# Attention kernel, one core: values of four heads in one go from a ring of five turned heads, and the inverse of the row sums spread on GpSimd

## The reference

```python
q, k, v = (proj(Wq), proj(Wk), proj(Wv))                   # x @ W.T, split into 16 heads of 32
scores = jnp.einsum('bhsd,bhtd->bhst', q, k) * D ** -0.5
scores = jnp.where(mask[None, None, :, :], -jnp.inf, scores)
attn = jax.nn.softmax(scores, axis=-1)
out = jnp.einsum('bhst,bhtd->bhsd', attn, v)
out = out.transpose(0, 2, 1, 3).reshape(B, S, E) @ Wo.T
xn = out / jnp.sqrt(jnp.mean(out * out, -1, keepdims=True) + EPS) * rms_scale
xn = xn * (1.0 + sc[:, None, :]) + shift[:, None, :]       # shift, sc from the condition
x = x + xn
x = x + x_rotated                                          # hamilton(q_left, hamilton(filtered x, conj q_right))
```

## Time and profile before

| | before |
|---|---|
| median of 3 runs | 988.27 us (987.57 to 989.47) |
| span of the profiled execution | 986.2 us |
| PE busy | 912.2 us (92%), 6278 matmuls |
| DVE busy | 707.5 us (72%) |
| ACT busy | 638.8 us (65%) |
| POOL busy | 523.6 us (53%) |
| mean granted TensorE clock | 0.979 |
| DMA | 153.98 MB, mean 156 GB/s |

### The profile page before, as it was taken

One profiled execution on the slowest core, in us unless ns is written; L12 is line 12 of the kernel. 1 busy time (PEld: TensorE's weight loads), 2 busy tenths in 40 slices (PEclk: granted clock), 3 DMA queues, 4 the chain that ended last, 5 costly groups with the idle time before them and its releaser, 6 DMA issues.

```text
span 986.2 us, 20466 instructions
## 1 busy us (share of the span) xinstructions
PE 912.2 (92%) x6278; PEld 648.2 (66%) x6278; DVE 707.5 (72%) x1581; ACT 638.8 (65%) x1523; POOL 523.6 (53%) x441
## 2 busy tenths in 40 slices
PE   7999999999968989999999998999999999999980
PEld 5788888888845557666666665666666666666650
DVE  4522132223168888989999898899999899898878
ACT  5222222223158888888888887788888888888820
POOL 0999930000001122677666776566677666776665
PEclk9999999999979999999999999999999999999995
DMA  8855465544878547756666745666665576455111
GB/s 282 303 188 193 170 223 189 183 171 181 186 249 185 118 98 181 164 117 151 150 140 139 194 108 129 152 155 145 142 161 125 133 187 156 109 120 139 33 54 43
DMA packets 82325, 153.98 MB, mean 156 GB/s; under 512 B 8472, under 2 KB 9112, under 8 KB 82224
## 3 DMA queue, kind: packets, MB, share of 16 engines
q1 hardware_dynamic: 82224, 152.75, 57.6%
HBM read 102.35 MB, written 50.36 MB: 155 GB/s over the span
## 4 chain that ended last, share of the span: by engine, by line
PE 59%; issue 6%; DVE 5%; POOL 1%; DVEq 0%; ACT 0%; POOLq 0%
PE prob_ps L663 27%; PE out_ps L679 15%; PE score_ps L647 12%; DVE probs_T L770 2%; PE y_ps L700 2%; PE y_ps L701 1%; PE y_ps L702 1%; PE out_ps L689 1%; DVE probs L528 1%; POOL probs L1008 1%; DVE probs L754 0%; DVE probs L824 0%; DVE probs L836 0%; DVEq L520 0%; DVE probs L831 0%
## 5 line engine op out<-in xcount | busy, mean ns | idle before, releaser
L867 ACT ACTIVATE probs<-probs,least 128x512 f32<-128x512 f32 x512 | 364.3, 716 | 32.0 <-DVE inv_den L763 25.4
L663 PE MATMUL prob_ps<-ident,probs 128*128 128x128 f32 x2048 | 314.5, 281 | 26.2 <-DVE probs_T L770 25.4
L754 DVE CUSTOM_DVE_ANT_0 probs<-score_ps,mask_bias 128x512 f32<-128x512 f32 x512 | 333.1, 679 | 4.4 <-PE score_ps L647 4.4
L663 PEld LDWEIGHTS prob_ps<-ident,probs 128*128 128x128 f32 x2048 | 227.4, 141 | 159.2 <-issue 117.7
L647 PE MATMUL score_ps<-k_rows,q_rows 128*128 128x512 f32 x512 | 240.4, 477 | 12.5 <-PEq L78 9.3
L770 DVE COPY probs_T<-prob_ps 128x512 f32<-128x512 f32 x256 | 175.4, 685 | 65.0 <-PE prob_ps L663 63.1
L874 ACT ACTIVATE probs_T<-prob_ps 128x512 f32<-128x512 f32 x256 | 153.2, 598 | 76.7 <-PE prob_ps L663 72.6
L271 DVE SCALAR_TENSOR_TENSOR late<-proj,late 128x512 fp32r<-128x512 f32 x64 | 44.0, 690 | 181.3 <-ACT late L240 181.2
L679 PE MATMUL out_ps<-probs_T,v_sb 128*32 128x256 f32 x2048 | 163.0, 391 | 0.0
L528 POOL TENSOR_TENSOR late<-rot,late 128x2048 f32<-128x2048 f32 x26 | 119.1, 4580 | 66.8 <-DVE late L787 66.8
L940 POOL TENSOR_TENSOR o_T<-raw_T 128x256 f32<-128x256 f32 x64 | 47.9, 748 | 142.3 <-ACT raw_T L882 142.3
(11 more groups left out here) (112 smaller groups left out, 1349.1 us busy)
## 6 DMA issues: line engine op xcount, KB each, us to landing
q_rows<-q_scratch SPq DMA_DIRECT2D x128, 256.0 KB, 5.8
k_rows<-k_scratch SPq DMA_DIRECT2D x128, 256.0 KB, 6.7
q_scratch<-late SPq DMA_DIRECT2D x64, 256.0 KB, 2.3
k_scratch<-late SPq DMA_DIRECT2D x64, 256.0 KB, 2.3
v_scratch<-v_out SPq DMA_DIRECT2D x32, 256.0 KB, 2.0
v_sb<-v_scratch SPq DMA_DIRECT2D x8, 1024.0 KB, 10.9
raw<-in_xT SPq DMA_DIRECT2D x7, 1024.0 KB, 5.6
late<-in_x SPq DMA_DIRECT2D x28, 256.0 KB, 2.7
```

Of the source, the lines that this page charges most:

```text
L663: last = pe.transpose(prob_ps[:, r % 2, j * HALF + c * P:j * HALF + (c + 1) * P], probs[:, s % 2, r // 2 * 2 + c, key:key + P], ident[:, :])
L754: dve.tensor_tensor_reduce(probs[:, s % 2, r, :], score_ps[:, r % 4, :], mask_bias[:, c, :], 1.0, 3e38, ALU.add, ALU.min, least[:, s % 2, ...
L867: act.activation(probs[:, s % 2, r, :], probs[:, s % 2, r, :], ACT.Exp, bias=least[:, s % 2, r:r + 1], scale=-1.0, accum_out=den[:, s % 2, ...
```

## The change

`attention` is written anew around whole units in place of half units.

- The tiles of a unit go head by head (n % 16 // 4 is the head, n % 4 the chunk), and `probs` is a ring of 12 tiles. A tile's transposes cover all 512 keys of its 128 queries as before, but the moved tiles go into `turned_probs`, a ring of five turned heads with all 512 queries each.
- The values of four heads are made in one go, 16 products of 512 columns, at tile 2 of the next unit, into a PSUM bank of their own (`value_ps`). Right behind them comes the scale's turning, four transposes, into a half of `turn_ps`, which it shares with the turned tiles (`place` gives the order of the halves).
- The reciprocal stays on DVE (L692 of after). Its spread goes to GpSimd (L863 of after). ACT moves the turned scale alone (L818 of after). DVE multiplies the values in PSUM by it (`norm`, L707 of after). GpSimd's multiplication goes; its cast and subtraction take 512 columns once per unit in place of 256 twice.
- Scores, masks and exponentials run 10, 6 and 4 tiles ahead. At tile 2 DVE and ACT take four tiles (`BURST`), and at tiles 4, 9 and 14 none (`SKIPS`).
- The projection's 12 products stand one to a tile, at tiles 3 to 14; a chunk is projected, squared, rescaled and rotated in other units than before.
- SP issues the loads of q and k rows first, then modulation or v, then store and x. The hardware loop is gone: all units are written out.
- The constant for the inverse root is one column in place of 256, and the tail has one rotation fewer on DVE.

```diff
+RING, SLOTS = 12, HG + 1
+SCORE_AHEAD, MASK_AHEAD, EXP_AHEAD = 10, 6, 4
+VALUE_AT, SCALE_AT, PROJECT_AT = 2, 2, 3
+NORM_AT, INVERT_AT, RESCALE_AT, RESIDUAL_AT, SQUARE_AT = 4, 0, 1, 2, 0
+BURST, SKIPS = 4, (4, 9, 14)
...
-        probs = sb("probs", [P, 2, TILES, S])
+        probs = sb("probs", [P, RING, S])
+        turned_probs = sb("turned_probs", [P, SLOTS, TC, S])
...
+            for u in range(U):
+                b, g = u // NG, u % NG
+                if u + 2 < U:
+                    load_unit(u + 2)
+                if g == 0:
+                    load_mod(b)
+                if g == 1 and b + 1 < B:
+                    load_v(b + 1)
+                if u >= NG + 2:
+                    store((u - NG - 2) // NG, (u - NG - 2) % NG)
+                if u >= NG:
+                    load_x(b - 1, g)
...
+            def turn(n):
+
+                pe.wait_ge(exped, n + 1)
+                place_free(pe, place(n) - 2)
...
+                for j in range(TC):
+                    for i in range(HG):
+                        h = HG * g + i
+                        last = pe.matmul(value_ps[i * D:(i + 1) * D, :], v_sb[:, b % 2, j, h * D:(h + 1) * D],
+                                         turned_probs[:, (HG * u + i) % SLOTS, j, :], start=(j == 0), stop=(j == TC - 1))
...
+            for n in range(N):
+                u, t = n // TILES, n % TILES
+                if t == VALUE_AT and u > 0:
+                    values(u - 1)
+                    turn_scale(u - 1)
+                if n + SCORE_AHEAD < N:
+                    score(n + SCORE_AHEAD)
+                if u >= NG and 0 <= t - PROJECT_AT < 12:
+                    project(u - NG, t - PROJECT_AT, y_ps[:, :])
+                turn(n)
...
+            def invert(u):
+                dve.wait_ge(exped, TILES * (u + 1))
+                if u > 0:
+                    dve.wait_ge(spread, u)
+                dve.reciprocal(inv[:, :, :], den[:, u % 2]).then_inc(inverted, 1)
...
+                dve.tensor_tensor(o_T[:, :], value_ps[:, :], inv_T[:, :], ALU.mult).then_inc(normed, 1)
...
+                if t == INVERT_AT and u > 0:
+                    invert(u - 1)
+                for _ in range(BURST if t == VALUE_AT else 0 if t in SKIPS else 1):
+                    if done < N:
+                        mask(done)
+                    done += 1
+                if t == RESCALE_AT and u > NG:
+                    rescale(u - NG - 1)
+                if t == RESIDUAL_AT and u > NG:
+                    residual(u - NG - 1)
+                if t == NORM_AT and u > 0:
+                    norm(u - 1)
+                if not by_act(n - 1) and n > 0:
+                    move_out(n - 1)
...
+                if t == SQUARE_AT and u > NG:
+                    square(u - NG - 1)
+                if t == SCALE_AT and u > 0:
+                    move_scale(u - 1)
+                if by_act(n - 1) and n > 0:
+                    move_out(n - 1)
...
+            def spread_inverse(u):
+                pool.wait_ge(inverted, u + 1)
+                if u > 0:
+                    pool.wait_ge(scale_turned, u)
+                pool.tensor_copy(inv_d[:, :, :, :], inv[:, :, :].rearrange("p i c -> p c i").unsqueeze(3)
+                                 .to_broadcast([P, TC, HG, D])).then_inc(spread, 1)
...
+            for u in range(U):
+                if u > 0:
+                    spread_inverse(u - 1)
+                if u > NG:
+                    rms(u - NG - 1)
+                if u > 0:
+                    split(u - 1)
+                if u > NG:
+                    rotate(u - NG - 1)
+                if u >= NG:
+                    shift(u - NG)
```

579 lines of the change are left out of this document (221 added, 358 removed).

## The result

The changed kernel takes 1018.07 us (median of 4 runs, 1015.9 to 1020.67) where the kernel before takes 988.75 (4 runs beside it): a ratio of 1.03, with a 95% interval of 1.0286 to 1.0314. It is slower, as forecast, but by 29 us where I had 13, and it ends just above the range. The span of the profiled execution is 1018.0 us (this execution took 1019.8), the mean granted clock 0.959 where it was 0.979.

The account below looks back on a forecast made before the run. TensorE was taken as the bound, with VectorE adding a stall per unit. Terms of -3, +15, -0.5 and +1.5 us made +13: a span of 999, with 2.1 us around it about 1001 us; range 963 to 1018.

Parts of the forecast that it names:

- The values: TensorE's value products in a unit, one run of four over 512 columns: 3.6 us plus 0.1 at the ends.
- the scale's move and the tile's behind it: Behind the scale, TensorE's next transpose waits for two ScalarE moves in a row: a stall of 1.1 us per unit.
- the rest of that unit's cycle: Everything in the loop from scale to next scale except x's landing, in units where x gates it: 6.9 us.
- the path forecast: Late x holds GpSimd's addition, that the spread, that TensorE's scale: units of 20.0 plain, 22.2 with modulation, 23.5 with v.
- The bare unit: A unit of four heads not held by x: falls only from 20.6 to 20.0 us, with 17.8 of TensorE's own work.
- the wait at the edge: Between units, the next first score waits for VectorE's move, inverse and mask: TensorE stalls 1.2 us.
- rival B: x gates the spread and TensorE's clock falls after idles; thirteen units lose up to 20 us: 1008 to 1021; chance 0.16.
- case A: Main case: x's late landing gates the spread, no loss of clock: 1001 us, range 992 to 1011; chance 0.50.
- units 4 to 28: Middle of attention, six batches of 85.9 us less 1.2: 514 us against 499.2 before, +15.
- The first four intervals: Attention up to unit 4, bound by VectorE's operations at about 19.1 us a unit: -3 us (from -6 to +3).
- What would show it: Listed trace signs: values run of 3.7 us, GpSimd waiting for x, scale held in two units per batch, wait behind the scale.
- The rule on completion order: DMA completion is not first in, first out per issuing engine; if x overtook, its queue terms would vanish.

Follow-up runs that it names:

- e1: Changed kernel with SyncE issuing the store and x ahead of the q and k loads and of modulation or v: 969.94 us.
- e2: Changed kernel with GpSimd's addition of the shift to x moved behind the spread and the inverse root: 976.79 us.
- e3: Changed kernel with store and x issued behind the q and k loads but ahead of modulation and v: 974.61 us.
- g1: Changed kernel with x first, masks 7 ahead, ScalarE moving the turned tile before the scale and, at the edge, tile 15 before its exponential and square: 915.49 us.
- e4: Changed kernel plus 34 filler transposes on TensorE ahead of the scale's wait for the spread, in six v units: 1010.1 us.
- f2: e1 with masks 7 tiles ahead, three tiles at tile 2 and tile 14 not skipped, for ScalarE's exponentials too: 966.84 us.
- h1: g1 with the scale again moved out ahead of the turned tile; x first, earlier masks and tile 15 first stay: 950.1 us.

## Why the prediction was wrong

**Right, term by term.** The values run in 3.64 us (3.6 forecast), the spread in 0.61 (0.65), the scale's move and the tile's behind it make 1.03 us of wait (1.1). x lands 17.1 us behind the loads in the v unit (16.6) and about 15.1 in the modulation unit (15.3), and the rest of that unit's cycle is 23.66 - 17.06 = 6.6 us (6.9); e1, e2 and e3 show that it acts mostly by the path forecast, addition, spread, scale. Modulation units took 130.9 us over six batches, as against 133.2, the fourth units 121.0 against 120.6. From the start of the last run of values to the end it is 1018.0 - 974.31 = 43.7 us, where it was 986.2 - 944.47 = 41.7 and 1.5 more were forecast.

**Right in sum, wrong in parts.** The bare unit is 20.04 us as forecast, but TensorE's own work in it is 18.2 (the busy 18.18, and all of the unit in g1), not 17.8, and the wait at the edge is 0.82, not 1.2. The two errors cancel, which is luck: 18.2 + 0.8 + 1.0.

**The step that failed is the clock, a term that the sum put at nothing.** It was written down as rival B, with the mechanism that came true, and given 0.16; the forecast's own case A had no term for it. The evidence against B was that idles of about 1 us had not slowed the clock. But the forecast itself put 2 to 3 us ahead of the scale and 1 us more behind it, and the only idle of that size in the trace, 3.25 us, had slowed it. The nearest row spoke for B, and I weighed the farther ones. B's size was about right: 19.0 us of additional busy time in the profiled execution against "up to 20". Here too two errors cancel: ten units of the changed kernel have a clock under 1.00, not thirteen, at some 1.9 us each and not 1.5. Seven of the ten cost 1.3 to 1.7 us, with a slow stretch of about 3.4 us (415.97 to 419.33, for one); the three from 500.69, 565.15 and 590.90 cost 2.4 to 2.9. In the sum of units 4 to 28 the third units of the batches took 131.2 us where six of 20.1 were forecast: +10.6. The v units took 144.1 against 139.8: +4.3, and nearly all of it is in the three that ran at a lower clock (25.75, 24.02 and 24.93 us); the three at 1.00 took 22.15, 23.66 and 23.58, where the first had no store ahead of x, against 22.3, 23.5 and 23.5. With modulation (-2.3) and fourth units (+0.4) that is the 13 us by which 527.2 exceeds 514. By experiment the clock's part is shown for the third units alone, 9.3 us in e4.

**Smaller misses.** The first four intervals were forecast at 4 x 19.1 and took 79.7, 3.3 us more: three are 19.42, where I had them bound by VectorE's operations (TensorE is busy 16.89 us in them, so 2.5 us are waits, and they fall to 18.2 us in g1), and the fourth is the first that waits for x, 21.5 us, which I counted only from the next on. What lies ahead of the first scale and behind the last makes 311.78 + 40.1 = 351.9 us; before it was 304.38 and, from 881.29 + 60.3 on, 44.6, so 349.0, and I had 0.2 taken off. (The 60.3 is 60.2 by the rows: 941.47 - 881.29.) That is 3.1 more, and no run here tells its cause; the last three intervals took 0.6 less. In all 13 + 3.3 + 3.1 - 0.6 = 19 us between the span of 999 and that of 1018.0. The median is 17 us above its forecast, since the profiled execution was 1.7 us slower than the median.

**The range** ended at 1018, inside B's own 1008 to 1021. The result stands 0.07 us above it.

**What would show it** named the signs rightly: the wait on x's DMA ahead of the addition, the scale held in the first two units of a batch, the wait behind the scale in every unit. The sign of units of 20, 20, 22 and 23.5 failed on the unit behind the v unit. The rule on completion order that the forecast cited from the Trainium skill (DMA: Bandwidth & Descriptors, Queues, rings and completion order) did not bring x ahead: in the rows above, x, issued last, landed 12.0 us after its issue, behind 1,024 KB of v.

**Not settled.** What idle slows the clock: at 565.15 a wait of 1.66 us ahead of the scale with 1.03 behind it did so, at 477.03 a wait of 1.60 with 1.03 did not, and no run isolates the point between them. Idles of about 1 us, which the forecast took as harmless, are not always so if two stand together. In e4, 0.89 us ahead of the scale and 1.04 behind it were followed by a score of 0.78 us, while 1.20 and 1.03 at 739.83 were not:

```profile
390.75 0.63 PE L626 MATMUL turn_ps<-ident,inv_d 128*128 128x128 f32 x4 [0.89 <-POOL inv_d L867]
...
392.65 0.99 PE L613 MATMUL turn_ps<-ident,probs 128*128 128x128 f32 x4 [1.04 <-ACT turned_probs L814]
393.29 0.78 PE L605 MATMUL score_ps<-k_rows,q_rows 128*128 128x512 f32 x1
```

Also open is why f2's unit is again 20.05 us though its two waits are 1.50 us and not 1.86. The busy time that rose by 0.36 fills it, and TensorE's weight loads wait 12.2 us in all for exponentials there, where it is 4.7 in e1 and 5.5 in h1, which keeps e1's exponentials and moves the tile first. No run took that apart.

## What to carry to other kernels

A load that was first in a queue and becomes last is a change in its own right: cost it by what then stands ahead of it in the queue, and follow its consumer's engine to whatever else was put behind that wait. Here this undid a gain that was there (969.94 us with x first, 915.49 with the orders of the engines changed as well). If a forecast puts TensorE idle for 2 us or more, look in the trace for an idle of that size, read the clock behind it, and put its price into the sum for every occurrence, not beside it; look at shorter idles too where two stand close together. And a wait at an edge where two engines hand over falls only when both do: take the second-latest into the sum before you claim the latest.
